# Scaled expert blocks scattered to the tokens' places by rows that carry their addresses, in a one-core fp32 attention and mixture-of-experts kernel

## The chip, the cores and the metric

The kernel runs on one core of a Trainium2 chip, as one launch. The metric is the device time in microseconds (us). A core has five engines that run side by side: TensorE (PE), VectorE (DVE), ScalarE (ACT), GpSimd (POOL) and SyncE (SP). They are ordered by semaphores alone. SP and ACT issue DMAs (rows named SPq and ACTq), and so does POOL, which also makes the indirect ones, whose row addresses come from a tile in SBUF.

## What is computed

Three residual layers on x of 16 x 64 tokens of width 512: cross attention to a context of 16 x 1601 rows, self attention with a low-rank correction, and a mixture of experts. The change is in the third:

```python
h = gelu(xf @ wg1 + bg1)                       # xf: the 1024 normalised tokens
probs = softmax((h @ wg2 + bg2)[:, :20])       # 20 experts
top_vals, top_idx = top_k(probs, 2)            # 2 experts for each token
gates = zeros((N, 20)).at[arange(N)[:, None], top_idx].set(top_vals)
def body(y, eb):
    We_e, be_e, g_e = eb
    return (y + g_e[:, None] * (xf @ We_e + be_e), None)
y, _ = scan(body, zeros, (We, be, gates.T))    # all in fp32
x = x + y
```

## The kernel before

All work of an engine is written out by hand in program order, with counted semaphores between the engines. Every fp32 product is made of three fp32r matmuls: an operand is split into a high part (an ACT copy) and a low part (a DVE subtraction, `rest` at L984 or `we_lo` at L1363), and `mm3` (L175 to L178) runs high-high, high-low and low-high.

**Cross attention** runs over the 16 batches in one pass (`cross`, 26.8 us a batch). SP loads the next batch's context into the single tile `craw` (L1650) as soon as DVE has read the former. Behind the context of batch 3, SP also clears two scratch tensors in HBM, `xg` and `yg` (4480 rows of 512 floats each): L1672 to L1677 write 20 pieces of 896 rows x 128 columns to `xg` and 12 pieces of 640 rows x 128 columns to the last rows of `yg`. The context of batch 4 stands behind them on SP's queue.

**Routing.** DVE picks two experts for each token, and its chain (L1384 to L1429) gives each of the 2 x 1024 (token, choice) pairs a slot: an expert n has the block of 128 slots n, and what does not fit goes to extra blocks, which 20 + `more` blocks hold in all (`more` is read from `ji`; in the profiled run there are 27 blocks). POOL then scatters the normalised token rows to their slots of `xg` by 16 indirect DMAs of 128 rows each (L1606), behind its low part of weight 2 (L1601).

**Expert blocks** (`block_of` on each engine). For block n, SP loads 128 token rows (`xi`, a ring of 6, L1754) and 1 MB of weights (`We`, a ring of 8 that runs ten blocks ahead, L1729 and L1732). PE transposes the rows of block n + 1 and then multiplies block n (12 matmuls of 512 columns). ACT does, in this order, the high part of the rows n + 1 (`xo`), the high part of the weights n + 2 (`we_hi`, 128 x 2048), the copy of the result n from PSUM to one of four buffers `yo` (in `xm` or `hT`), and issues its DMA to the block's 128 rows of `yg` (L963). DVE makes the two low parts; that of the weights, `we_lo`, reads two tiles of SBUF. POOL has nothing to do in this stage.

**The end.** All five engines meet at a barrier once the last stores have landed. POOL gathers each token's two result rows from `yg` by 16 indirect DMAs (L1624) into a ring `yga` of four tile pairs, DVE scales each by its gate and adds it to `x_sb` (L1478, L1481), and SP stores eight tiles of the result (L1795).

Of the kernel before, what the change touches and what calls it, by code (L numbers as in the profile page):

```python
# [17 lines left out]
def perceiver(nc, t, out):  # L18
# [5 lines left out]
    R, X, EARLY = 8, 6, 4  # L24
# [3 lines left out]
    with root:  # L28
# [3 lines left out]
        def sb(name, shape, dt=f32, es=root):  # L32
# [12 lines left out]
        acc = sb("acc", [128, NB, 8, 32])  # L45
        acct = acc[:, :, :, :].rearrange("p b t c -> p b (t c)")
        nm = sb("nm", [128, NB, 8])
        ls = sb("ls", [128, NB, 8])
# [73 lines left out]
        mf = sb("mf", [128, 8, 8])  # L122
# [12 lines left out]
        jc = sb("jc", [1, 15, E])  # L135
        jf = sb("jf", [1, 16])
        ji = sb("ji", [1, 16], i32)
        cs2 = sb("cs2", [128, 660])
        wr = sb("wr", [128, 6, 4, D])
        xi = sb("xi", [128, 6, D])  # L140
        xall = acc[:, :, :, :].rearrange("p b t c -> p (b t c)").rearrange("p (i n) -> p i n", i=8)
        p2 = [xall[:, 4:6, :].rearrange("p i n -> p (i n)").rearrange("p (t b k) -> p t b k", t=8, b=2), p2b[:, :, :, :]]
        bvr, g1raw = xall[:, 7, :], xall[:, 6, :].rearrange("p (k n) -> p k n", k=4)
        yo = [xm[:, 0, :], xm[:, 1, :], hT[:, 0:D], hT[:, D:T]]
        yga = wr[:, 0:2].rearrange("p r (a c) n -> p (r a) c n", c=2)
# [16 lines left out]
            v_gt p_gT v_gT p_be v_y d_sc a_we v_we a_wx v_wx p_xo a_xo v_xo p_y a_y v_out d_out  # L162
# [5 lines left out]
        d_ga = [sem(f"d_ga{i}") for i in range(4)]  # L168

        d_x, d_w = (S["d_x0"], S["d_x1"]), (S["d_w0"], S["d_w1"])  # L170
# [64 lines left out]
        def tensor(pe):  # L235
# [142 lines left out]
            pe.wait_ge(S["d_lora"], 16)  # L378
# [76 lines left out]
            weight_lora(0, 1, (d_raw[1], 16))  # L455
            pe.wait_ge(S["d_bro"], 16)
# [19 lines left out]
            weight_lora(1, 1, (d_raw[1], 32))  # L476
# [53 lines left out]
            def dense(what, i):  # L530
# [99 lines left out]
            pe.drain().then_inc(S["s_bar"], 1)  # L630
            pe.wait_ge(S["s_bar"], 2 * BARRIER)
# [18 lines left out]
        def bank_of(what, i):  # L650
            return bank[what, i]
# [26 lines left out]
        def scalar(act):  # L678
# [42 lines left out]
            def cross(seg):  # L721
                for n in range(16 * seg, 16 * seg + NB + 1):
# [46 lines left out]
            weight_hi(wh[0], raw[:, 0], (d_w[0], 16))  # L769
# [3 lines left out]
            weight_hi(wk, raw[:, 1], (d_w[1], 16))  # L773
            weight_hi(wv, raw[:, 0], (d_w[0], 32))
# [51 lines left out]
            def norm(n, i, dst):  # L826
                act.wait_ge(S["g_r"], n + 1)
                if n >= 12:
                    act.wait_ge(S["p_t2"], 14)
# [28 lines left out]
            act.wait_ge(d_raw[0], 32)  # L858
# [7 lines left out]
            act.wait_ge(d_raw[0], 48)  # L866
# [81 lines left out]
            def block_of(n):  # L948
# [27 lines left out]
            act.drain().then_inc(S["s_bar"], 1)  # L976
            act.wait_ge(S["s_bar"], 2 * BARRIER)


        def vector(dve):  # L980
# [22 lines left out]
            dve.wait_ge(S["d_m"], 32)  # L1003
# [52 lines left out]
            def make_cap(seg):  # L1056
                dve.wait_ge(S["d_cap"], 48 * (seg + 1))
# [831 lines left out]
```

## Time and profile before

| what | value |
|---|---|
| device time, median of 3 runs (lowest to highest) | 886.27 us (883.11 to 887.11) |
| device time of the profiled execution | 883.6 us |
| span of the profiled execution | 881.7 us |
| mean granted TensorE clock | 0.939 |
| PE, DVE, ACT, POOL busy | 764.9, 438.1, 386.8, 357.3 us |
| DMA traffic | 94.07 MB, mean 107 GB/s |

The span runs from the first to the last instruction of the profiled execution; 1.9 us of its device time lie outside. An engine's busy time is the sum over stages that are bound by different things, so a stage has to be looked at by itself. The stages: cross attention to about 522 us, self attention to about 702, routing and the scatter to about 751, expert blocks to about 850, the end to 881.7.

### The profile page before, as it was taken

How to read it: one execution, taken by the hardware profiler on the slowest of the kernel's cores; microseconds unless marked ns; L12 is line 12 of the kernel's file. 1: busy time of each engine (PE TensorE's matmuls, PEld its weight loads, DVE VectorE, ACT ScalarE, POOL GpSimd, SP SyncE). 2: the span in 40 equal slices, each digit the busy share in tenths (PEclk: the TensorE clock that was granted, in tenths of full speed). 3: DMA queues.
4: the chain of work that ended last, by engine and by line, in shares of the span. 5: the costliest groups of instructions: out<-in, count | busy, mean ns of one | idle time of the engine just before them, and what ended most of it. 6: DMA issues, size and time to landing. Idle time of an engine off the chain costs nothing.

```text
span 881.7 us, 16368 instructions
## 1 busy us (share of the span) xinstructions
PE 764.9 (87%) x6435; PEld 624.0 (71%) x6435; DVE 438.1 (50%) x907; ACT 386.8 (44%) x680; POOL 357.3 (41%) x367
## 2 busy tenths in 40 slices
PE   1999999889999999999999769799998537799950
PEld 0888888768888788887888557678887432687740
DVE  5724443444444444444444327434687363388844
ACT  1444552544444545445443414642344420488830
POOL 1228653754577545775455407300235127000025
PEclk9999999999999999999999989899999955799985
DMA  9201598221021110111100001101000474599837
GB/s 300 84 1 40 163 285 228 88 87 35 7 88 39 41 38 3 41 40 40 39 3 2 1 17 49 48 13 49 2 2 1 191 304 178 183 413 420 356 110 237
DMA packets 47862, 94.07 MB, mean 107 GB/s; under 512 B 3195, under 2 KB 29691, under 8 KB 43295
## 3 DMA queue, kind: packets, MB, share of 16 engines
q1 hardware_dynamic: 41326, 77.43, 25.1%
q0 software_dynamic: 2560, 8.39, 2.9%
q10 hardware_dynamic: 3888, 7.08, 2.1%
q8 instruction: 55, 0.90, 0.4%
q14 instruction: 33, 0.26, 0.1%
HBM read 66.41 MB, written 26.48 MB: 105 GB/s over the span
## 4 chain that ended last, share of the span: by engine, by line
PE 68%; ACT 7%; DVE 6%; SPq 5%; DMA 5%; issue 5%; POOL 3%; ACTq 1%; PEld 0%; POOLq 0%; DVEq 0%; PEldq 0%
PE bank L176 17%; PE bank L178 15%; PE bank L177 15%; PE bank L182 8%; SPq L1674 5%; PE bank L292 5%; PE bank L318 3%; ACT wh L680 3%; DMA xi<-scratch_xg 2%; PE bank L494 2%; POOL scratch_xg L1606 1%; ACT xu L680 1%; DMA wr<-scratch_yg,si 1%; POOL wr L1624 1%; PE bank L417 1%
## 5 line engine op out<-in xcount | busy, mean ns | idle before, releaser
L1532 POOL TENSOR_SCALAR pp<-pp,rl 128x416 f32<-128x416 f32 x128 | 190.4, 1501 | 174.2 <-DVE rl L1078 174.1
L1162 DVE CUSTOM_DVE_ANT_0 pp<-bank,cap 128x416 f32<-128x416 f32 x128 | 70.5, 589 | 106.2 <-PE bank L292 106.2
L754 ACT ACTIVATE pp<-pp,nm 128x416 f32<-128x416 f32 x128 | 81.2, 635 | 45.6 <-DVE nm L1162 45.3
L984 DVE TENSOR_TENSOR kk<-bank,kk 128x416 fp32r<-128x416 f32 x64 | 37.9, 592 | 124.8 <-ACT kk L680 124.8
L176 PE MATMUL bank<-chi,wk 128*128 128x416 f32 x256 | 95.5, 373 | 0.0
L177 PE MATMUL bank<-clo,wk 128*128 128x416 f32 x256 | 90.1, 352 | 0.0
L178 PE MATMUL bank<-chi,wk 128*128 128x416 f32 x256 | 90.1, 352 | 0.0
L176 PE MATMUL bank<-wv,chi 128*128 128x512 f32 x208 | 87.7, 422 | 0.0
L178 PE MATMUL bank<-wv,clo 128*128 128x512 f32 x208 | 82.2, 395 | 0.0
L177 PE MATMUL bank<-wv,chi 128*128 128x512 f32 x208 | 81.8, 393 | 0.0
L680 ACT ACTIVATE kk<-bank 128x416 fp32r<-128x416 f32 x64 | 33.1, 517 | 98.8 <-PE bank L178 98.8
L176 PE MATMUL bank<-wh,xu 128*128 128x512 f32 x152 | 63.7, 419 | 8.1 <-issue 4.7
L182 PE MATMUL bank<-cst,pp 128*128 128x128 f32 x512 | 68.5, 277 | 0.0
L182 PEld LDWEIGHTS bank<-cst,pp 128*128 128x128 f32 x512 | 57.8, 141 | 7.2 <-issue 3.3
L680 ACT ACTIVATE xu<-bank 128x512 fp32r<-128x512 f32 (+1 forms) x60 | 31.0, 541 | 72.1 <-PE bank L182 48.1
L177 PE MATMUL bank<-wh,xu 128*128 128x512 f32 x152 | 60.8, 400 | 0.0
L178 PE MATMUL bank<-wh,xu 128*128 128x512 f32 x152 | 60.7, 400 | 0.0
L1624 POOL DMA_INDIRECT wr<-scratch_yg,si x16 | 17.0, 1063 | 107.8 <-SPq L1791 103.3
L680 ACT ACTIVATE pt<-bank 128x512 f32<-128x512 f32 x64 | 38.0, 594 | 50.1 <-PE bank L182 50.1
L1132 DVE COPY pt<-bank 128x512 f32<-128x512 f32 x64 | 43.9, 686 | 22.6 <-PE bank L182 22.6
L176 PEld LDWEIGHTS bank<-wv,chi 128*128 128x128 f32 x208 | 39.4, 189 | 21.0 <-issue 14.4
L680 ACT ACTIVATE vv<-bank 128x512 f32<-128x512 f32 x52 | 31.0, 596 | 46.2 <-PE bank L178 46.2
(228 smaller groups left out, 1606.9 us busy)
## 6 DMA issues: line engine op xcount, KB each, us to landing
wr<-in_We SPq DMA_DIRECT2D x19, 1024.0 KB, 11.1
craw<-in_ctx SPq DMA_DIRECT2D x16, 832.0 KB, 4.4
scratch_xg<-zero SPq DMA_DIRECT2D x20, 448.0 KB, 6.3
raw<-in_We SPq DMA_DIRECT2D x8, 1024.0 KB, 11.3
xi<-scratch_xg SPq DMA_DIRECT2D x28, 256.0 KB, 10.1
scratch_yg<-zero SPq DMA_DIRECT2D x12, 320.0 KB, 5.2
scratch_yg<-xm ACTq DMA_DIRECT2D x14, 256.0 KB, 7.0
scratch_yg<-hT ACTq DMA_DIRECT2D x13, 256.0 KB, 6.6
```

Source lines behind the costliest of these rows:

```text
L176: pe.matmul(o, lhs[0], rhs[0], start=start, stop=False)
L177: pe.matmul(o, lhs[0], rhs[1], start=False, stop=False)
L178: return pe.matmul(o, lhs[1], rhs[0], start=False, stop=stop)
L182: last = pe.transpose(bank[0:n, k * 128:(k + 1) * 128], of(k), ident)
L292: last = pe.matmul(pb[3 + u][:, 0:CW], q[r, s, g, :], w[r, g, :], start=start, stop=stop)
L680: return act.activation(dst, src, ACT.Copy)
L754: act.activation(frame(p8), frame(p8), ACT.Exp, bias=bias, scale=-1.0, accum_out=total).then_inc(S["a_exp"], 1)
L984: return dve.tensor_tensor(dst, src, hi.bitcast(f32), ALU.subtract)
L1132: dve.tensor_copy(pt[:, p8 % 4, :, :].rearrange("p a c -> p (a c)"), pb[5][:, :]).then_inc(S["v_pt"], 1)
L1162: dve.tensor_tensor_reduce(out=frame(p8), in0=pb[3 + p8 % 2][:, 0:CW], in1=cap[:, :], scale=-1.0, scalar=nm[:, b, p8:p8 + 1] if seg else 3 ...
L1532: pool.tensor_scalar(frame(p8), frame(p8), rl[:, n % 2, p8:p8 + 1], None, ALU.mult).then_inc(S["g_pn"], 1)
L1674: sp.dma_start(t[name][first_ * 128:(first_ + n_) * 128, k * 128:(k + 1) * 128].rearrange("(a p) n -> p a n", p=128), zero[:, :].unsqueeze ...
```

## The change

- A row of `xg` and of the tile `xi` has 520 floats in place of 512. The eight more hold the token's two experts, its two gates, the two rows of the result at which its two products belong, and (for a slot that no token fills) a row of its own beyond the result's.
- `yg` goes; `ys` has 2048 rows for the 2 x 1024 products and 4480 behind them for the empty slots. The 12 clearing pieces for `yg` go. In their place one DMA from HBM to HBM writes the eight columns of 4480 rows of `xg` from a prepared array `empty`.
- For each block, POOL works out the gate and the row of each of its 128 tokens from the eight columns in five small instructions (`address`).
- ACT multiplies by the gate when it evicts the block from PSUM, and no longer stores. POOL stores, by an indirect DMA that scatters the 128 rows to `ys`.
- The barrier at the end goes, and so do the 16 gathers. SP waits for the last four scatters and then issues eight loads of 2 x 128 contiguous rows; DVE adds them without a factor.
- Several tiles of the self attention move within `acc`, because the eight token tiles there are now 520 wide, and some semaphores are shared. The instructions are otherwise the same.

```diff
-    R, X, EARLY = 8, 6, 4
+    R, X, EARLY, RW = 8, 6, 4, D + 8
...
-        yga = wr[:, 0:2].rearrange("p r (a c) n -> p (r a) c n", c=2)
+        yga = wr[:, 0:4].rearrange("p r (a c) n -> p (r a) c n", c=2)
...
# scalar, block_of(n)
-                copy(yo[n % 4], pb[3 + n % 2][:, :]).then_inc(S["a_y"], 1)
-                act.wait_ge(S["a_y"], n + 1)
-                act.dma_start(t["yg"][n * 128:(n + 1) * 128, :], yo[n % 4]).then_inc(d_yo[n % 4], 16)
+                act.wait_ge(S["g_ad"], n + 1)
+                act.activation(yo[n % 4], pb[3 + n % 2][:, :], ACT.Identity,
+                               scale=gd[:, n % 4, 0:1]).then_inc(S["a_y"], 1)
...
# vector, routing
-            chain(dve.tensor_copy(mf[:, :, :], mi[:, :, :]))
+            dve.wait_ge(S["d_gate"], 32)
+            dve.tensor_copy(xrow[:, :, D + 2:D + 4], mg[:, :, 0:2])
+            dve.tensor_copy(xrow[:, :, D + 4:D + 7], place_of)
+            chain(dve.tensor_copy(xrow[:, :, D:D + 2], mi[:, :, 0:2]))
...
# vector, the end
-                r = i % 4
-                dve.wait_ge(d_ga[r], 32 * (i // 4 + 1))
-                dve.scalar_tensor_tensor(out=x_sb[:, i, :], in0=yga[:, r, 0, :], scalar=mg[:, i, 0:1],
-                                         in1=x_sb[:, i, :], op0=ALU.mult, op1=ALU.add).then_inc(S["v_out"], 1)
...
+                dve.wait_ge(d_ga[i], 16)
+                for c in range(2):
+                    if c:
+                        dve.wait_ge(S["v_out"], 2 * i + 1)
+                    dve.tensor_tensor(x_sb[:, i, :], x_sb[:, i, :], yga[:, i, c, :], ALU.add).then_inc(S["v_out"], 1)
...
# gpsimd
+            def address(n):
...
+                r = n % X
+                pool.wait_ge(d_xi[r], 16 * (n // X + 1))
+                own.on(pool.tensor_scalar(eq[:, :], xi[:, r, D:D + 2], float(n) if n < E else jf[:, n - E:n - E + 1], None,
+                                          ALU.is_equal))
+                pool.wait_ge(own.sem, own.n)
+                own.on(pool.tensor_tensor(ad[:, :, :], xi[:, r, D + 2:D + 6].rearrange("p (a c) -> p a c", a=2),
+                                          eq[:, :].unsqueeze(1).to_broadcast([128, 2, 2]), ALU.mult))
+                pool.wait_ge(own.sem, own.n)
+                own.on(pool.tensor_tensor(gd[:, n % 4, :], ad[:, :, 0], ad[:, :, 1], ALU.add))
+                pool.wait_ge(own.sem, own.n)
+                own.on(pool.tensor_tensor(gd[:, n % 4, 1:2], gd[:, n % 4, 1:2], xi[:, r, D + 6:D + 7], ALU.add))
+                pool.wait_ge(own.sem, own.n)
+                if n >= 4:
+                    pool.wait_ge(d_yo[n % 4], 16 * (n // 4))
+                pool.tensor_copy(di[:, n % 4:n % 4 + 1], gd[:, n % 4, 1:2]).then_inc(S["g_ad"], 1)
+
+            def block_of(n):
+                address(n + 1)
+                pool.wait_ge(S["g_ad"], n + 1)
+                pool.wait_ge(S["a_y"], n + 1)
+                pool.indirect_dma_start(out=t["ys"][:, :],
+                                        out_offset=bass.IndirectOffsetOnAxis(ap=di[:, n % 4:n % 4 + 1], axis=0),
+                                        in_=yo[n % 4], in_offset=None).then_inc(d_yo[n % 4], 16)
...
# sync, cross attention
-        cleared = [("xg", 7 * j, 7) for j in range(5)] + [("yg", E + 5 * j, 5) for j in range(3)]
+        cleared = [(7 * j, 7) for j in range(5)]
...
+                        sp.dma_start(t["xg"][:, D:RW], t["empty"]).then_inc(S["d_z"], 16)
...
# sync, load_tokens(n) and the end
+                    sp.wait_ge(S["g_ad"], n - X + 1)
...
-            sp.drain().then_inc(S["s_bar"], 1)
-            sp.wait_ge(S["s_bar"], 2 * BARRIER)
+
+            for i in range(8):
+                sp.dma_start(yga[:, i], t["ys"][0:2 * T, :].rearrange("(c i p) n -> i p c n", c=2, i=8)[i]).then_inc(
+                    d_ga[i], 16)
```

On SP's queue in the cross attention, around the clearing, before:

```order
L1650 ISA
L1650 DMA craw<-in_ctx 128x1664
L1674 DMA scratch_xg<-zero 128x7x128 x20
L1674 DMA scratch_yg<-zero 128x5x128 x12
L1650 ISA
L1650 DMA craw<-in_ctx 128x1664
```

and in the changed kernel:

```order
L1677 ISA
L1677 DMA craw<-in_ctx 128x1664
L1701 DMA scratch_xg<-zero 128x7x128 x20
L1705 DMA scratch_xg<-in_empty 4480x8
L1677 ISA
L1677 DMA craw<-in_ctx 128x1664
```

Twelve pieces have left, one DMA of 4480 rows of 8 floats has come, and the context load of batch 4 follows it.

On POOL, from the scatter of the tokens on; the names in brackets are the semaphores that an instruction waits for (d_xi: the token rows have landed, g_ln: POOL's own last instruction, a_y: ACT's eviction, g_ad: `address`). Before:

```order
L1606 DMA scratch_xg<-acc,si 4480x512 x15
L1610 TENSOR_LOAD ji [waits v_ji]
L1610 ISA x2
L1612 COMPARE_AND_BRANCH x15
L1616 UNCONDITIONAL_BRANCH
L1624 DMA wr<-scratch_yg,si 128x512 [waits s_bar]
L1624 DMA wr<-scratch_yg,si 128x512 x7
```

and in the changed kernel, to the scatter of block 0:

```order
L1611 DMA scratch_xg<-acc,si 4480x520 x15
L1615 TENSOR_LOAD ji [waits v_ji]
L1615 ISA x2
L1623 TENSOR_SCALAR eq<-xi 128x2 [waits d_xi0]
L1626 TENSOR_TENSOR ad<-xi,eq 128x4 [waits g_ln]
L1629 TENSOR_TENSOR gd<-ad 128x2 [waits g_ln]
L1631 TENSOR_TENSOR gd<-gd,xi 128x1 [waits g_ln]
L1635 CAST di<-gd 128x1 [waits g_ln]
```

```order
L1623 TENSOR_SCALAR eq<-xi 128x2 [waits d_xi1]
L1626 TENSOR_TENSOR ad<-xi,eq 128x4 [waits g_ln]
L1629 TENSOR_TENSOR gd<-ad 128x2 [waits g_ln]
L1631 TENSOR_TENSOR gd<-gd,xi 128x1 [waits g_ln]
L1635 CAST di<-gd 128x1 [waits g_ln]
L1641 DMA scratch_ys<-xm,di 6528x512 [waits a_y,g_ad]
```

The first five of these instructions are `address(0)`, the next six are what every block then has: the address of block n + 1 and the scatter of block n.

On ACT, the first blocks (p_y: PE has finished the block, d_we: weights have landed), before:

```order
L680 ACTIVATE xm<-bank 128x512 [waits v_slot,p_y]
L963 DMA scratch_yg<-xm 128x512 [waits a_y]
L680 ACTIVATE xu<-bank 128x512 [waits p_y,p_xo]
L680 ACTIVATE wh<-wr 128x2048 [waits p_y,d_we3]
L680 ACTIVATE xm<-bank 128x512 [waits v_slot,p_y]
L963 DMA scratch_yg<-xm 128x512 [waits a_y]
```

and in the changed kernel:

```order
L969 ACTIVATE xm<-bank,gd 128x512 [waits g_ad,v_slot,p_y]
L683 ACTIVATE xu<-bank 128x512 [waits p_y,p_xo]
L683 ACTIVATE wh<-wr 128x2048 [waits p_y,d_we3]
L969 ACTIVATE xm<-bank,gd 128x512 [waits g_ad,v_slot,p_y]
L683 ACTIVATE xu<-bank 128x512 [waits p_y,p_xo]
```

The DMA has left ACT, and the eviction waits for POOL's `address` as well.

## Rows read from the trace of the kernel before

**Rows 1.** The page, part 4: the chain that ended last, share of the span by engine.

```profile
PE 68%; ACT 7%; DVE 6%; SPq 5%; DMA 5%; issue 5%; POOL 3%; ACTq 1%; PEld 0%; POOLq 0%; DVEq 0%; PEldq 0%
```

**Rows 2.** Timeline of SP's queue, 86 to 205 us: start, us, engine, line, operation, count.

```profile
98.31 30.70 SPq L1674 DMA_DIRECT2D scratch_xg<-zero  x20
129.06 15.11 SPq L1674 DMA_DIRECT2D scratch_yg<-zero  x12
```

**Rows 3.** Stage table: window, length, busy (count) PE, PEld, DVE, ACT, POOL, clock, DMA, GB/s.

```profile
109.60:136.40 26.80, 26.80 (x273) 22.45 (x269) 11.81 (x31) 13.08 (x28) 16.39 (x17) 1.00 1.04 287
136.40:167.70 31.30, 28.64 (x274) 23.98 (x269) 11.86 (x31) 12.60 (x28) 16.35 (x17) 0.95 0.60 184
```

**Rows 4.** Critical chain, 90 to 170 us: start, us, what; the context of batch 4.

```profile
144.35 7.33 DMA craw<-in_ctx
```

**Rows 5.** ACT's waits, 90 to 170 us: waiting, waited for, us in total, times, longest.

```profile
ACT chi L680 <- DMA craw<-in_ctx: 8.3, 1, 8.3
```

**Rows 6.** Timeline of ACT, from the first eviction of a block on.

```profile
760.94 0.60 ACT L680 ACTIVATE xm<-bank 128x512 f32<-128x512 f32 x1 [4.67 <-PE bank L178]
...
765.86 1.90 ACT L680 ACTIVATE wh<-wr 128x2048 fp32r<-128x2048 f32 x1
...
768.28 0.33 ACTq L963 DMA_DIRECT2D scratch_yg<-hT  x1
```

**Rows 7.** Critical chain, 700 to 882 us: DVE's cast, last scatter, last eviction, last addition.

```profile
717.13 3.47 DVE mf L1389
...
748.19 2.69 DMA scratch_xg<-acc,si
...
849.15 0.61 ACT hT L680
...
878.51 0.75 DVE x_sb L1481
```

**Rows 8.** Timeline of DVE, 782 to 800 us: the low parts of two weights.

```profile
784.52 2.29 DVE L1363 TENSOR_TENSOR wh<-raw,wh 128x2048 fp32r<-128x2048 f32 x1 [0.45 <-ACT wh L680]
...
787.87 2.29 DVE L1363 TENSOR_TENSOR wh<-wr,wh 128x2048 fp32r<-128x2048 f32 x1 [0.45 <-ACT wh L680]
```

**Rows 9.** Stage table of two stretches of the expert blocks.

```profile
782.00:815.00 33.00, 33.00 (x160) 26.26 (x159) 28.49 (x21) 28.80 (x30) 0.00 (x0) 1.00 1.03 418
833.00:850.00 17.00, 16.11 (x80) 12.88 (x78) 11.43 (x9) 11.17 (x13) 0.00 (x0) 1.00 0.28 104
```

**Rows 10.** Timeline of PE, 815 to 834 us: the token transposes and their waits.

```profile
825.16 0.66 PE L182 MATMUL bank<-cst,xi 128*128 128x128 f32 x4 [0.34 <-DMA xi<-scratch_xg]
...
828.93 0.66 PE L182 MATMUL bank<-cst,xi 128*128 128x128 f32 x4 [0.36 <-DMA xi<-scratch_xg]
```

**Rows 11.** Line 1568, a POOL operation: ns min/median/max, first and last start.

```profile
L1568 POOL TENSOR_TENSOR nbias<-nbias,rstd x16: 189/189/603, 534.6 to 701.2; 128x1 f32<-128x1 f32 x16
```

**Rows 12.** Timeline of DVE and POOL, 640 to 646 us, around the longest of those.

```profile
643.97 0.55 POOL L1567 TENSOR_TENSOR rstd<-rstd,cst 128x1 f32<-128x1 f32 x1 [1.16 <-DVE nbias L1238]
644.47 0.68 DVE L984 TENSOR_TENSOR g<-acc,g 128x512 fp32r<-128x512 f32 x1
644.60 0.60 POOL L1568 TENSOR_TENSOR nbias<-nbias,rstd 128x1 f32<-128x1 f32 x1
```

**Rows 13.** Timeline of POOL and DVE, 846 to 882 us: two of the 16 gathers.

```profile
857.28 0.75 DVE L1478 SCALAR_TENSOR_TENSOR x_sb<-wr,mg,x_sb 128x512 f32<-128x512 f32 x1 [9.11 <-DMA wr<-scratch_yg,si]
857.47 1.38 POOL L1624 DMA_INDIRECT wr<-scratch_yg,si  x1 [0.30 <-issue]
...
864.43 0.94 POOL L1624 DMA_INDIRECT wr<-scratch_yg,si  x1 [0.30 <-issue]
864.78 0.75 DVE L1478 SCALAR_TENSOR_TENSOR x_sb<-wr,mg,x_sb 128x512 f32<-128x512 f32 x1 [3.17 <-DMA wr<-scratch_yg,si]
```

**Rows 14.** DMA issues of the span: form, count, KB each, median us to landing.

```profile
craw<-in_ctx SPq DMA_DIRECT2D x16, 832.0 KB, 4.4
```

More of the change, by code:

```diff
@@ L44, in perceiver @@
         iota20 = cst[:, 160:180]
[L45 to L48, printed above, removed]
+        acc = sb("acc", [128, NB * 256 + 2 * NB * 8])
+        acct = acc[:, 0:NB * 256].rearrange("p (b n) -> p b n", b=NB)
+        nm, ls = [acc[:, NB * 256 + j * 128:NB * 256 + (j + 1) * 128].rearrange("p (b h) -> p b h", b=NB)
+                  for j in range(2)]
         raw = sb("raw", [128, 2, 4, D])
@@ L167, in perceiver @@
         d_yo = [sem(f"d_yo{i}") for i in range(4)]
-        d_ga = [sem(f"d_ga{i}") for i in range(4)]
-        d_x, d_w = (S["d_x0"], S["d_x1"]), (S["d_w0"], S["d_w1"])
+        d_ga = [sem(f"d_ga{i}") for i in range(8)]
+        d_x = (S["d_x0"], S["d_x1"])
         d_raw = (S["d_raw0"], S["d_raw1"])
@@ L827, in norm @@
                 act.wait_ge(S["g_r"], n + 1)
-                if n >= 12:
+                if n == 11:
+                    act.wait_ge(S["v_v2"], 8)
+                elif n == 12:
+                    act.wait_ge(S["v_g1"], 1)
+                elif n >= 13:
                     act.wait_ge(S["p_t2"], 14)
@@ L1418, in vector @@
                                             op1=ALU.add))
-            chain(dve.tensor_tensor(jc[:, :, :], ob[0:1, 20:40].unsqueeze(1).to_broadcast([1, 15, E]),
+            chain(dve.tensor_tensor(jc[:, :, :], ob[:, 20:40].unsqueeze(1).to_broadcast([128, 15, E]),
                                     jg.rearrange("p (j e) -> p j e", e=E), ALU.is_le))
@@ L1429, in vector @@
             dve.tensor_copy(si[:, :, :], sf[:, :, :]).then_inc(S["v_slot"], 1)
-            own.on(dve.tensor_scalar(ji[:, 0:15], jf[:, 0:15], float(E - 1), None, ALU.min))
+            chain(dve.tensor_scalar(jf[:, 0:15], jf[:, 0:15], float(E - 1), None, ALU.min))
+            own.on(dve.tensor_copy(ji[:, 0:15], jf[0:1, 0:15]))
             dve.wait_ge(own.sem, own.n)
@@ L1607, in gpsimd @@
                                             out_offset=bass.IndirectOffsetOnAxis(ap=si[:, c, i:i + 1], axis=0),
-                                            in_=xall[:, i, :], in_offset=None).then_inc(S["d_sc"], 16)
+                                            in_=xrow[:, i, :], in_offset=None).then_inc(S["d_sc"], 16)
             pool.wait_ge(S["v_ji"], 1)
             more = pool.value_load(ji[0:1, 15:16], min_val=0, max_val=X8)
+            def address(n):
+                if n >= LAST:
+                    return
+                r = n % X
[20 more added lines that the diff above has]
+                                        in_=yo[n % 4], in_offset=None).then_inc(d_yo[n % 4], 16)
+            address(0)
+            for n in range(E):
+                block_of(n)
             for j in range(X8):
@@ L1613, in gpsimd @@
                 guards[-1].__enter__()
[L1614 removed]
+                block_of(E + j)
             while guards:
                 guards.pop().__exit__(None, None, None)
[L1617 to L1629 removed]
+        cleared = [(7 * j, 7) for j in range(5)]
+        Z_ALL = 16 * (4 * len(cleared) + 1)
         def sync(sp):
@@ L1841 @@
     cs2[:, 360:660] = _np.repeat(_np.arange(15), 20)
+    place = cs2[:, 660:684].reshape(128, 8, 3)
+    for c in range(2):
+        place[:, :, c] = _np.arange(128)[:, None] + 128 * _np.arange(8) + 1024 * c
+    empty = _np.zeros((35 * 128, 8), _np.float32)
+    empty[:, 6] = 2048 + _np.arange(35 * 128)
     wqkv, bqkv = v["L0_attn_w_qkv"], v["L0_attn_b_qkv"]
```

103 lines of the change are left out of this document (44 added, 59 removed).

## The prediction

> **What bounds the kernel now.** I read the chain that ended last first, then the stages it passes. TensorE holds 68% of it [rows 1], but the change leaves TensorE's work as it is, so I look for the places where the chain leaves PE. There are three: 5% of the span on SP's queue, the expert blocks, and the end.
>
> *The clearing.* SP issues 20 pieces to xg in 30.7 us and 12 to yg in 15.1 us [rows 2], and the DMA engines are full meanwhile (share 1.04 at 287 GB/s [rows 3]). The context of batch 4 is issued behind them at 144.35 and lands 7.33 us later, at 151.7 [rows 4]; ACT waits 8.3 us for it [rows 5]. PE loses less: that batch takes 31.3 us against 26.8 for its neighbour [rows 3], that is 4.5. So 8.3 - 4.5 = 3.8 us of such a delay cost PE nothing.
>
> *The expert blocks.* The first eviction starts at 760.94 [rows 6], the last at 849.15 [rows 7]: 26 intervals in 88.2 us, 3.39 each. Two limits lie on top of each other. ACT and DVE set a pace of 3.35 (the two weight operations of rows 8 start that far apart). And a block moves 1.05 MB of weights, 0.26 of tokens and 0.26 of results, 1.57 MB; at the 418 GB/s of full DMA engines [rows 9] that is 3.76 us, the pace at which PE's transposes wait for tokens late in the stage (825.16 to 828.93 [rows 10]). Weights loaded ahead hide that limit for two thirds of the blocks. PE alone could do 3.22: 80 matmuls, five blocks, in 16.11 us [rows 9].
>
> *The end* takes 881.7 - 849.15 - 0.6 = 32.0 us from the last eviction's end.
>
> **Part 1, the clearing.** The 20 xg pieces have 20 x 896 = 17,920 rows of 512 bytes, 1.71 ns each at 30.7 us. The new DMA adds 4480 rows of 32 bytes. The trace has no such transfer. Lower bound: by its bytes nothing; nearest row: the same 1.71 ns a row, 7.7 us; upper bound: twice that, 15.4, because it both reads and writes HBM. The xg rows are now 2080 bytes apart, which may slow their 512-byte pieces, by nothing to a quarter (estimate). With the nearest row, SP is through at 98.3 + 30.7 + 7.7 = 136.7, and the context lands, 7.3 us later as before [rows 4], at 144.0. It would cost PE nothing up to 151.7 - 4.5 = 147.2. Gain 4.5, and no more is to be had there. Upper end: 98.3 + 38.4 + 15.4 = 152.1, 7.8 later than before, all of it paid: 7.8 lost. I take -4.5, since 3.2 us of reserve are left. The Trainium skill, DMA: Bandwidth & Descriptors, Specifications, speaks against this: below 512 bytes the DMA engine does a read-modify-write. It gives no price for one, and no row here shows it; the sum by it would be that of the upper end.
>
> **Part 2, routing.** DVE's cast took 3.47 us [rows 7] because POOL's subtraction for weight 2 was under way; the two new small copies stand in front of it and partly vanish in that wait. Bounds 0 to 0.5; I take +0.4, two small DVE operations. The extra waits of moved tiles are for events that lie steps back: nothing.
>
> **Part 3, the expert blocks.** ACT loses a DMA issue of 0.33 us [rows 6] and its wait, so its pace drops from 3.35 to about 2.95, below PE's 3.22. That gives at most what DMA leaves, for the last weights still arrive at DMA's pace: 0 to -1. What comes is POOL's work. A small operation takes 0.19 [rows 11], and the next that depends on it starts 0.08 after its end (643.97 + 0.55 = 644.52 to 644.60 [rows 12]); I take 0.25 for each of the five, so `address` takes 1.25. A scatter takes 0.30 + 0.96 = 1.26 like the gathers [rows 13]. Sum 2.5, under 3.22: were POOL alone, it would hide. It isn't. In rows 12 a POOL operation begun while DVE works on two SBUF tiles ends at 645.20, just after DVE (645.15), in 0.60 instead of 0.19. In rows 13 an indirect DMA begun under such a DVE operation (to 858.03) ends 0.82 later, while one that has begun 0.35 us before DVE is not disturbed. So each of POOL's six starts needs a moment in which DVE isn't in a two-tile operation; `we_lo` is one, and lasts 2.29 per block [rows 8].
>
> Bounds for the pace. Best phase: only the scatter's 0.82 lies under `we_lo`; 2.29 + 1.25 + 0.15 = 3.7. Worst: nothing does; 2.5 + 2.3 = 4.8. What does the program do? Say POOL finishes an `address` at 0 and ACT has waited for it. ACT evicts (0.5), copies rows (0.5) and the weights (1.9, all three by rows 6, the small ones overlapping by 0.1): `we_lo` runs from 3.0 to 5.3. POOL scatters to 1.3 and makes the next address by 2.55 (a short block: ACT takes it up at 3.0). The next scatter starts at 2.85, before DVE, and is done at 3.8. Then the address after next: its first operation is held to 5.3, the others follow, but the next `we_lo` is due at 6.0, when three or four are done, and holds the rest to 8.3; the address is ready at about 8.6. Two blocks take 8.6, 4.3 each. From there it repeats. The first three intervals have little of this: 3 x 3.2 + 23 x 4.3 = 108.5 against 88.2: **+20.3**. Ends: 3.7 gives 94.7 (+6.5), 4.8 gives 120 (+32). DMA isn't the limit at 4.3 (1.57 MB in 4.3 us is 366 GB/s). Queued behind POOL's wait is only POOL; those who wait for it are ACT's eviction, then PE's third block after, through the two result banks.
>
> **Part 4, the end.** After the last eviction POOL may still have to scatter the block before, make an address and scatter the last: 1.3 to 3.8, I take 3.2. Landing 0.3 + 2.7, from the scatter to xg [rows 7]. Eight loads: 512 KB land first after about 3.6 (832 KB take 4.4 [rows 14]); all 4.2 MB need 10.0 at 418 GB/s, so DVE's 16 additions at 0.72 (0.68 [rows 12] and a wait), 11.5, end last. The last store takes 881.7 - 879.26 = 2.4 [rows 7]. Sum 3.2 + 3.0 + 0.3 + 3.6 + 11.5 + 2.4 = 24.0: **-8.0**, range -5 to -10. Hidden: the barrier, and the loads behind the additions.
>
> **Sum**: -4.5 + 0.4 + 20.3 - 8.0 = +8.2. The profiled 883.6 (1.9 outside its span) becomes 891.8. The median of the runs is 2.7 above that execution, so 886.3 + 8.2 = 894.5.
>
> **Rivals.**
> *POOL hides.* If the small operations slip between DVE's, POOL's 2.5 stays under 3.22 and DMA sets the end of the stage: -0.5 there, and the last scatter starts at once, -9.9 at the end. Sum -14.5: 871.8. For it: the sum of 2.5, and an idle DVE for 1 us a block. Against: rows 12 and 13. It decides for the gain from a POOL chain of about 0.7 us on, where I have 1.25.
> *Best phase.* The pace settles at 3.7: +6.5. Sum -5.6: 880.7.
> *No overlap at all.* Pace 4.8, +32, sum +20: 906. The Trainium skill, SBUF — State Buffer, section "SBUF: two separate sides", says that GpSimd cannot write descriptors while DVE holds the shared port in a two-port mode. Were it so for `we_lo` too, the 0.82 could not lie under it and this rival would hold; the undisturbed issue of rows 13 says otherwise.
> *The clearing runs late.* The upper end of part 1, on top of the forecast: +7.8 in place of -4.5, 906.8. It decides from an SP queue that is through later than 139.9.
>
> **Chances.** Forecast (pace 4.0 to 4.6, 887 to 902) 0.50; POOL hides 0.20; best phase 0.12; no overlap 0.08; late clearing 0.10. A measurement can tell about 0.5%, 4.4 us. Faster: the 0.20 and most of the 0.12, 0.31. The same: some 0.14 of the forecast's lower edge and the rest, 0.15. Slower: 0.54. The range leaves out about 0.15 and takes in the hidden POOL's edge and both late ends: 870 to 908. The likeliest case's own is 887 to 902.
>
> **What the new profile should show.** SP through with the clearing near 137 and no wait of ACT for the context. In the expert blocks POOL near full, its small operations in two kinds (0.19, and up to 2.3 when held), evictions alternating between about 3 and 5.7 us, ACT waiting for POOL, DMA share under 1. The end 24 us long, with DVE adding without gaps. An even pace near 3.4 with no ACT wait for POOL would prove part 3 wrong; a context that lands after 147 proves part 1 wrong.

## The result, and the profile after

The changed kernel takes 907.8 us (median of four runs, 904.7 to 911.4), the kernel before 886.7 beside it: a ratio of 1.025, with a 95% interval of 1.019 to 1.031. Two of the four runs lie near 905 and two near 911; nothing here shows what separates them, and the profile is of the fastest. The profiled execution took 904.7 us with a span of 902.9, against 883.6 and 881.7. The prediction was 894.5: the right side, but a growth of 8.2 us where 21 were measured, at the upper edge of the range. The two spans differ by 21.2 us. To find where, I cut both at the first and the last eviction of an expert block:

| stretch of the span, us | before | after | difference | forecast |
|---|---|---|---|---|
| up to the first eviction | 760.94 | 757.66 | -3.3 | -4.1 |
| first to last eviction, 26 intervals | 88.2 | 119.5 | +31.3 | +20.3 |
| start of the last eviction to the end | 32.6 | 25.7 | -6.8 | -8.0 |

**The chain.** The page of after, part 4. GpSimd (POOL) stood at 3% of it before [rows 1]:

```profile
PE 71%; POOL 13%; issue 6%; DVE 5%; DMA 2%; ACT 2%; PEld 0%; POOLq 0%; SPq 0%; DVEq 0%; PEldq 0%; ACTq 0%
```

**The clearing.** Timeline of SP's queue in after (start, us, engine, line, operation, count), and the stage of the batch behind it (window, length, busy and count of PE, PEld, DVE, ACT, POOL, then PE's granted clock, DMA share and GB/s):

```profile
98.14 34.05 SPq L1701 DMA_DIRECT2D scratch_xg<-zero  x20
132.24 1.65 SPq L1705 DMA_DIRECT2D scratch_xg<-in_empty  x1
134.08 4.61 SPq L1677 DMA_DIRECT2D craw<-in_ctx  x1
```

```profile
135.70:162.20 26.50, 26.50 (x264) 22.19 (x255) 11.83 (x30) 12.79 (x29) 16.09 (x16) 1.00 0.43 114
```

SP is through at 133.9. ACT's wait of 8.3 us for the context [rows 5] is gone, and the batch takes 26.5 us where it took 31.3 [rows 3].

**The expert blocks.** Timeline of DVE, ACT and POOL in after, two blocks from one free scatter to the next. L1641 is the scatter, L1623 to L1635 the five address steps, L1368 the low part of a weight (`we_lo`), L969 the eviction:

```profile
837.87 1.08 POOL L1641 DMA_INDIRECT scratch_ys<-xm,di  x1 [0.52 <-POOL di L1635]
838.53 1.91 ACT L683 ACTIVATE xu<-wr 128x2048 fp32r<-128x2048 f32 x1
...
839.03 0.21 POOL L1623 TENSOR_SCALAR eq<-xi 128x2 f32<-128x2 f32 x1
...
840.13 0.18 POOL L1635 CAST di<-gd 128x1 uint32<-128x1 f32 x1
...
840.43 0.69 ACT L969 ACTIVATE hT<-bank,gd 128x512 f32<-128x512 f32 x1
840.47 2.29 DVE L1368 TENSOR_TENSOR xu<-wr,xu 128x2048 fp32r<-128x2048 f32 x1 [1.11 <-ACT xu L683]
840.83 2.89 POOL L1641 DMA_INDIRECT scratch_ys<-xm,di  x1 [0.52 <-POOL di L1635]
...
843.44 2.29 DVE L1368 TENSOR_TENSOR wh<-wr,wh 128x2048 fp32r<-128x2048 f32 x1
843.79 2.01 POOL L1623 TENSOR_SCALAR eq<-xi 128x2 f32<-128x2 f32 x1
...
846.70 0.18 POOL L1635 CAST di<-gd 128x1 uint32<-128x1 f32 x1
847.00 0.69 ACT L969 ACTIVATE hT<-bank,gd 128x512 f32<-128x512 f32 x1 [3.59 <-POOL di L1635]
847.40 1.08 POOL L1641 DMA_INDIRECT scratch_ys<-hT,di  x1 [0.52 <-POOL di L1635]
```

A scatter that starts before `we_lo` takes 1.08 us. The one at 840.83 starts 0.36 us after `we_lo` began, and takes 2.89: it ends 0.96 us after DVE does. The compare at 843.79 starts 0.35 us after the next `we_lo`, and takes 2.01 instead of 0.21. Undisturbed, POOL gets from one scatter to the next in 2.96 us (837.87 to 840.83), and disturbed in 6.57. The pair is 9.53, or 4.77 a block; with two easy intervals at the start and a cheaper pair at the end the mean is 4.60. ACT waits for POOL's address meanwhile, in 11 long waits of together 39.6 us (waiting, waited for: us in total, times, longest):

```profile
ACT hT L969 <- POOL di L1635: 21.6, 6, 3.7
ACT xm L969 <- POOL di L1635: 18.0, 5, 3.7
```

The stage table of a longer stretch, with PE's clock at 0.95, shows that no other resource is full: POOL is busy for 52.8 of 65 us, and the rest are the gaps within its own cycle (0.52 before the scatter and five of about 0.08, 0.90 in each of 13.6 cycles). PE has 50.7, and DMA is at 0.88 where it was 1.03 [rows 9].

```profile
782.00:847.00 65.00, 50.71 (x224) 39.69 (x224) 40.48 (x28) 39.74 (x41) 52.84 (x82) 0.95 0.88 307
```

**The end**, timelines of ACT, POOL, SP's queue and DVE in after:

```profile
877.18 0.69 ACT L969 ACTIVATE hT<-bank,gd 128x512 f32<-128x512 f32 x1 [1.86 <-POOL di L1635]
...
880.60 1.08 POOL L1641 DMA_INDIRECT scratch_ys<-hT,di  x1 [0.52 <-POOL di L1635]
...
887.52 10.81 DVE L1487 TENSOR_TENSOR x_sb<-x_sb,wr 128x512 f32<-128x512 f32 x16 [11.49 <-DMA wr<-scratch_ys]
```

```profile
883.63 4.01 SPq L1822 DMA_DIRECT2D wr<-scratch_ys  x8
```

The 16 additions run without gaps, as forecast, and end at 898.3; 4.6 us pass from there to the end of the span, when the last store has landed.

### The profile page after: what moved, and what is told of

Read it like the earlier page. It is cut to its first block, busy times and chain, and to the rows that moved or that the text cites. A ratio compares the mean times of both kernels' runs of the same rounds, so it can differ in the third digit from the quotient of the medians.

```text
span 902.9 us, 16536 instructions
## 1 busy us (share of the span) xinstructions
PE 770.3 (85%) x6435; PEld 627.9 (70%) x6435; DVE 437.9 (49%) x910; ACT 389.1 (43%) x680; POOL 442.0 (49%) x518
## 3 DMA queue, kind: packets, MB, share of 16 engines
q1 hardware_dynamic: 40126, 77.97, 26.7%
## 4 chain that ended last, share of the span: by engine, by line
PE 71%; POOL 13%; issue 6%; DVE 5%; DMA 2%; ACT 2%; PEld 0%; POOLq 0%; SPq 0%; DVEq 0%; PEldq 0%; ACTq 0%
PE bank L181 18%; PE bank L183 16%; PE bank L182 16%; PE bank L187 8%; POOL scratch_ys L1641 5%; PE bank L297 5%; PE bank L323 3%; POOL eq L1623 3%; PE bank L499 2%; POOL scratch_xg L1611 2%; DVE x_sb L1487 1%; PE bank L422 1%; POOL gd L1629 1%; PE bank L511 1%; PE bank L529 1%
## 5 line engine op out<-in xcount | busy, mean ns | idle before, releaser
L757 ACT ACTIVATE pp<-pp,acc 128x416 f32<-128x416 f32 x128 | 81.3, 636 | 47.7 <-DVE acc L1167 47.5
L181 PE MATMUL bank<-wh,xu 128*128 128x512 f32 x152 | 64.5, 424 | 22.3 <-DVE xu L989 12.5
L989 DVE TENSOR_TENSOR xu<-bank,xu 128x512 fp32r<-128x512 f32 (+1 forms) x60 | 35.7, 613 | 54.2 <-ACT xu L683 54.1
L1137 DVE COPY pt<-bank 128x512 f32<-128x512 f32 x64 | 43.9, 686 | 25.7 <-PE bank L187 25.7
```

Source lines behind the costliest of these rows:

```text
L181: pe.matmul(o, lhs[0], rhs[0], start=start, stop=False)
L757: act.activation(frame(p8), frame(p8), ACT.Exp, bias=bias, scale=-1.0, accum_out=total).then_inc(S["a_exp"], 1)
L989: return dve.tensor_tensor(dst, src, hi.bitcast(f32), ALU.subtract)
L1137: dve.tensor_copy(pt[:, p8 % 4, :, :].rearrange("p a c -> p (a c)"), pb[5][:, :]).then_inc(S["v_pt"], 1)
```

## The experiments

Two theories stood after the traces. **T**: POOL's own cycle is the pace of the expert blocks, 2.96 us by itself and some 1.8 more for each `we_lo` that it runs into. **Rivals**: the length of POOL's chain without any hold, the landing of scatters and weights, or the hand-over between POOL and ACT. All spans are cut as above. Each ratio is to runs of the kernel before that were made beside that kernel; their medians are 886.7 for after, 884.3 for e1 to e4, 886.4 for e5 to e7 and 884.1 for e8 to e10. The changed kernel was not run again beside the experiments, so differences from it carry some 2 to 3 us of doubt.

| kernel | median us | ratio to before (95%) | 26 intervals | mean | last eviction to end |
|---|---|---|---|---|---|
| before | 886.7 | | 88.2 | 3.39 | 32.6 |
| after | 907.8 | 1.025 (1.019 to 1.031) | 119.5 | 4.60 | 25.7 |
| e1, low part from PSUM | 872.6 | 0.986 (0.983 to 0.989) | 88.3 | 3.40 | 24.3 |
| e2, low part in four | 876.2 | 0.990 (0.987 to 0.993) | 89.6 | 3.44 | 25.7 |
| e3, clearing part alone | 881.5 | 0.997 (0.995 to 0.999) | 88.2 | 3.39 | 34.3 |
| e4, addresses worked out once | 871.8 | 0.985 (0.983 to 0.988) | 87.5 | 3.37 | 23.7 |
| e5, address two ahead | 904.9 | 1.023 (1.020 to 1.025) | 116.4 | 4.48 | 28.3 |
| e6, e1 with four more steps | 892.0 | 1.009 (1.005 to 1.012) | 104.0 | 4.00 | 26.8 |
| e7, e1 for even blocks alone | 883.4 | 0.998 (0.995 to 1.000) | 96.5 | 3.71 | 26.7 |
| e8, e4 again | 871.3 | 0.985 (0.983 to 0.988) | 87.3 | 3.36 | 24.2 |
| e9, e4 with the low part in four | 870.9 | 0.985 (0.983 to 0.987) | 87.1 | 3.35 | 24.1 |
| e10, e4 with stores by ACT | 873.4 | 0.987 (0.984 to 0.989) | 87.3 | 3.36 | 25.6 |

### e1: the hold taken away, the work kept

```diff
+                if n < 3:
...
+                    return
-                dve.tensor_tensor(wsplit[n % 3][1], wraws[n % R], wsplit[n % 3][0].bitcast(f32),
+                dve.tensor_tensor(wsplit[n % 3][1], wraws[n % R],
+                                  pb[7][:, :].unsqueeze(1).to_broadcast([128, 4, D]),
                                   ALU.subtract).then_inc(S["v_we"] if n < E else S["v_wx"], 1)
```

> The changed kernel, with one operand of VectorE's low-part instruction moved out of SBUF: from the fourth weight on it reads a PSUM bank where it read the high part in SBUF (so the low parts are wrong numbers; size and count of the work are as before). In the changed kernel a GpSimd instruction that touches SBUF while that 2.29 us instruction runs takes 2.0 to 2.9 us instead of 0.2 to 1.1. Theory (the two engines hold each other up at SBUF, and the scatter starts 0.36 us after the low part begins instead of before it): no GpSimd row of the expert blocks above 1.3 us, blocks at 3.2 to 3.6 us each instead of 4.60, the 26 intervals shorter by 26 to 36 us, total 870 to 880. Rival A (the length of GpSimd's own chain of seven dependent steps, 3.5 us when nothing holds it, plus the hand-overs, sets the pace): 4.3 to 4.6, total 898 to 906. Rival B (scatter landings or the weight loads set it): no change, 903 to 911.

Blocks take 3.40 us in the mean, as before, and the total is 35 us below the changed kernel's. One address and its scatter in e1, and the `we_lo` (now L1372) that runs meanwhile, timeline of POOL and DVE:

```profile
802.26 0.21 POOL L1628 TENSOR_SCALAR eq<-xi 128x2 f32<-128x2 f32 x1
...
802.67 2.29 DVE L1372 TENSOR_TENSOR wh<-raw,bank 128x2048 fp32r<-128x2048 f32 x1 [0.32 <-ACT wh L683]
...
803.35 0.18 POOL L1640 CAST di<-gd 128x1 uint32<-128x1 f32 x1
804.32 1.08 POOL L1646 DMA_INDIRECT scratch_ys<-hT,di  x1 [0.78 <-ACT hT L969]
```

`we_lo` is as long as before, 2.29 us, and only one of its inputs has changed its place. No POOL row is long, neither the cast nor the scatter that start under it, and the scatter now waits for ACT, not the other way round. POOL's 28 chains are all still there, so their length alone isn't the cause; nor are the landings. Rivals A and B fall. The mean of 3.40 is made of blocks of 3.2 and, late in the stage, seven of 3.7 to 4.4, where before had 3.34 and then up to 3.77.

### e2: the same work in shorter instructions

```diff
+                for k in range(4):
+                    ins = dve.tensor_tensor(wsplit[n % 3][1][:, k, :], wraws[n % R][:, k, :],
+                                            wsplit[n % 3][0][:, k, :].bitcast(f32), ALU.subtract)
+                ins.then_inc(S["v_we"] if n < E else S["v_wx"], 1)
```

> The changed kernel, with the low part (2.29 us for 128x4x512) issued as four instructions of 128x512, about 0.6 us each; nothing else. Theory (GpSimd is held until the running VectorE instruction ends): it then waits at most 0.6 us at a time, a scatter takes at most 1.7 us and the compare at most 0.9, pace 3.5 to 4.0, total 876 to 892. If VectorE keeps the port across instructions that stand back to back, the holds stay at 1.8 us and nothing changes: 903 to 911. Rival (GpSimd's chain or the landings): 903 to 911 too, but with short rows.

One held scatter and one held step of e2:

```profile
800.44 1.34 POOL L1643 DMA_INDIRECT scratch_ys<-hT,di  x1 [0.52 <-POOL di L1637]
...
802.19 0.51 POOL L1628 TENSOR_TENSOR ad<-xi,eq 128x4 f32<-128x4 f32 x1
```

The holds shrink from 1.8 us to mostly 0.3 or 0.4 (0.7 at most), the blocks to 3.44, just under the range expected: between two DVE instructions that stand back to back POOL gets its turn. Four pieces take 2.50 us where one took 2.29. This version does all the work, and it is 1.0% faster than the kernel before (876.2 against 884.3).

### e3: the clearing part alone

```diff
                     if seg == 0 and b == 2:
-                        for name, first_, n_ in cleared:
+                        for name, first_, n_ in cleared[0:5]:
...
+                    if seg == 0 and b == 12:
+                        for name, first_, n_ in cleared[5:8]:
```

> The kernel before, with the twelve zero pieces of the result scratch issued after the fourteenth context load instead of in one row with the other twenty after the fourth. They are as many, and the rest is the kernel before. The changed kernel is without them, and its first 757 us came out 3.28 us shorter than before (6.24 us at 442 us, of which about 3 were lost again at the end of cross attention, where TensorE's granted clock dipped). Theory (they stand before the fifth context load on SyncE's queue and nothing else notices them): 4 to 6.5 us shorter at 442 us, total 880 to 884. Rival (the gain needs the pieces gone, because their transfer takes the same room wherever it stands): within 1 us of the kernel before, 883 to 888.

Moved, the twelve pieces cost nothing where they now are (timeline of SP's queue in e3):

```profile
377.34 13.68 SPq L1681 DMA_DIRECT2D scratch_yg<-zero  x12
```

Two rows of PE, the first product of the output projection, of before and of e3, show what it gives:

```profile
498.74 0.50 PE L176 MATMUL bank<-wh,oh 128*128 128x512 f32 x1 [2.80 <-DVE oh L984]
```

```profile
495.06 0.50 PE L176 MATMUL bank<-wh,oh 128*128 128x512 f32 x1 [2.79 <-DVE oh L984]
```

It is 3.7 us, a little less than the 4 expected, and 4.5 if one allows for e3's context load, which SP issued 0.8 us later than before's (98.75 against 97.93). The profiled execution keeps little of it: its first eviction is 1.5 us earlier than before's, since 2.1 are lost in front of the row scatters (see the last section), and 1.7 more are lost at the end (34.3 against 32.6), in code that is the same. It is the slowest of ten runs. The median falls by 2.8, and the interval of the ratio (0.995 to 0.999) leaves out 1: the rival falls, by a small margin.

### e4: the whole chain taken off GpSimd

```diff
+            act.wait_ge(S["d_sc"], 256)
+            act.dma_start(ex[:, :, :], t["xg"][:, D:RW].rearrange("(n p) c -> p n c", p=128)).then_inc(S["d_ex"], 16)
...
+            chain(dve.tensor_tensor(eq[:, :, :], ex[:, :, 0:2], bid[:, :].unsqueeze(2).to_broadcast([128, NBK, 2]),
+                                    ALU.is_equal))
...
             def block_of(n):
-                address(n + 1)
-                pool.wait_ge(S["g_ad"], n + 1)
                 pool.wait_ge(S["a_y"], n + 1)
                 pool.indirect_dma_start(out=t["ys"][:, :],
```

The multiplication, the two additions and the cast follow in the same manner, each once for all 35 blocks. The loads of the token rows leave out the eight columns and no longer wait for POOL, so e4 changes more than one thing at once; the single cause rests on e1 and e5 to e7.

> The changed kernel with gates and places worked out once: one load brings the eight extra columns of all 35 blocks after the row scatters, VectorE computes all gates and places in five small instructions, and GpSimd only scatters. The block loads leave the extra columns out. Theory (GpSimd's chain under the hold sets the pace): 35 fewer chains of 1.0 to 3 us; a scatter may still be held behind a low part (2.9 us), but nothing stands behind it any more, so blocks at 3.2 to 3.5 us, first eviction later by 1 to 3 us (the extra load of about 2 us and some 1.5 us on VectorE), total 870 to 880. Rival A (the scatter's hold itself sets the pace): 4.0 or more, total above 888. Rival B (landings): 4.6, 903 to 911.

Timelines of DVE and of POOL in e4:

```profile
757.46 0.31 DVE L1483 TENSOR_TENSOR jc<-hT,sl 128x140 f32<-128x140 f32 x1
757.80 0.23 DVE L1485 TENSOR_TENSOR gd<-jc 128x70 f32<-128x70 f32 x1
```

```profile
781.53 1.99 POOL L1639 DMA_INDIRECT scratch_ys<-hT,di  x1 [1.20 <-ACT hT L973]
784.71 1.99 POOL L1639 DMA_INDIRECT scratch_ys<-xm,di  x1 [1.20 <-ACT xm L973]
787.90 1.99 POOL L1639 DMA_INDIRECT scratch_ys<-xm,di  x1 [1.20 <-ACT xm L973]
```

The five instructions take 1.2 us for all blocks together, behind a wait of 2.1 us for their load. The scatter is still held, to 1.8 or 2.0, in nearly every block, and yet the blocks come every 3.19 us here, since POOL has 1.2 us to spare behind it. Rival A falls. At 871.8 us this is 36 us below the changed kernel and 12.5 below the kernel before beside it.

### e5: the same steps, one block earlier

```diff
-                if n >= 4:
-                    pool.wait_ge(d_yo[n % 4], 16 * (n // 4))
+                if n >= 8:
+                    pool.wait_ge(d_yo[n % 4], 16 * (n // 4 - 1))
...
-                address(n + 1)
+                address(n + 2)
```

> The changed kernel with the address steps two blocks ahead of their scatter instead of one (rings of eight for gates and places, one more token load at the end); the same instructions. Two theories agree so far. Theory T (throughput): GpSimd's own cycle is the pace. Without holds one cycle is 2.93 us (scatter 1.08, five small steps with their gaps 1.35, 0.5 from the last step to the next scatter), and each cycle or so meets one low part and loses up to 1.8: twice 2.93 and two holds of 1.8 are 9.5 us a pair, and 9.54 was measured. Then working further ahead changes little: 4.3 to 4.8 a block, total 896 to 911. Theory L (hand-over): ScalarE's wait for the address of the next block (39.6 us in 11 waits) closes a loop, and working two ahead opens it: 3.3 to 3.7 a block, total 871 to 882.

T's side: 904.9 us, 4.48 a block. Timeline of POOL in e5:

```profile
803.75 2.89 POOL L1641 DMA_INDIRECT scratch_ys<-xm,di  x1 [0.52 <-POOL di L1635]
...
807.29 2.19 POOL L1629 TENSOR_TENSOR gd<-ad 128x2 f32<-128x2 f32 x1
```

Another step is hit, but for as long, and the mean falls by 0.12 only. POOL isn't late by its place in a loop: its cycle and the holds fill the time.

### e6: the cycle made longer without a hold

```diff
+                for _ in range(2):
+                    own.on(pool.tensor_scalar(eq[:, :], xi[:, r, D:D + 2], float(n) if n < E else jf[:, n - E:n - E + 1], None,
+                                              ALU.is_equal))
+                    pool.wait_ge(own.sem, own.n)
...
```

> The kernel of the first experiment (low part from PSUM, so no holds; its low parts are wrong numbers), with the first four of the five address steps done twice. That adds four times 0.27 us, 1.1 us a block, to GpSimd and no hold. Theory T: GpSimd's cycle is 2.93 + 1.1 = 4.0, above the 3.4 of the rest, so 4.0 to 4.2 a block and a total of 888 to 895, against 872.6 of the first experiment. If only being held matters and length doesn't (the rest has room): 3.4 and 871 to 875.

Measured 892.0 and 4.00 us a block. Two scatters of e6 stand 4.07 apart:

```profile
799.83 1.08 POOL L1647 DMA_INDIRECT scratch_ys<-hT,di  x1 [0.53 <-POOL di L1641]
...
803.90 1.08 POOL L1647 DMA_INDIRECT scratch_ys<-hT,di  x1 [0.52 <-POOL di L1641]
```

So length counts as a hold does, once the sum exceeds what the rest needs (3.2 to 3.8 in e1).

### e7: the hold in every second block

```diff
-                if n < 3:
+                if n < 3 or n % 2:
```

> The kernel of the first experiment with the PSUM operand for even blocks alone; the odd ones read the SBUF high part again (low parts of the even ones are wrong numbers). Theory T: a pair costs twice 2.93 and one hold of 1.8 at most, 7.7 us, so 3.6 to 3.9 a block where it starved before and a total of 877 to 886. If the first hold of a pair is what sets off the second (phase), taking one away takes both: 3.4 and 871 to 876.

Measured 883.4 and 3.71 a block. Timeline of POOL in e7, one cycle free (2.95) and one held (4.77), 7.72 the pair, as expected:

```profile
802.60 1.08 POOL L1646 DMA_INDIRECT scratch_ys<-hT,di  x1 [0.52 <-POOL di L1640]
...
805.55 2.90 POOL L1646 DMA_INDIRECT scratch_ys<-xm,di  x1 [0.52 <-POOL di L1640]
...
810.32 1.07 POOL L1646 DMA_INDIRECT scratch_ys<-xm,di  x1 [0.52 <-POOL di L1640]
```

With e1, e6, e7 and the changed kernel the price adds up: 2.96 + 0 stays hidden, 2.96 + 1.1 gives 4.00, half a hold 3.71, a hold in each cycle 4.60 (means of 26; in the steady part 4.07, 3.86 and 4.77).

### e8 to e10: what is left in the batched kernel

> The batched kernel of the fourth experiment once more, on the chip and beside the two that follow, to compare them with. 871.8 us was measured; 869 to 874 again.

871.3 us; it repeats.

e9 has the edit of e2 on top of e4.

> The batched kernel with the low part in four instructions of 128x512. In the batched kernel a scatter is still held by 0.9 us in every block (about 1.9 to 2.0 against 0.96 us), but GpSimd has 1.2 to 1.9 us to spare behind it. Theory T (a hold costs something only where GpSimd's cycle is the longest): scatters of 1.2 us or less, and the total unchanged within 1.5 us, or up to 2 us longer, since the four pieces take 2.50 us where one took 2.29. If the hold itself still costs in the batched kernel: 2 to 6 us shorter.

870.9 us, the same. The scatters are short, 1.00 for most and up to 1.47 for the others, somewhat above the 1.2 expected:

```profile
793.63 1.00 POOL L1641 DMA_INDIRECT scratch_ys<-hT,di  x1 [2.19 <-ACT hT L973]
```

That a hold off the path costs nothing is thus shown twice, in e4 and here.

```diff
-            for i in range(8):
-                sp.wait_ge(S["v_out"], 2 * i + 2)
-                sp.dma_start(out.rearrange("(i b) q d -> i (b q) d", b=2)[i], x_sb[:, i, :]).then_inc(S["d_out"], 16)
...
+            for i in range(8):
+                act.wait_ge(S["v_out"], 2 * i + 2)
+                act.dma_start(out.rearrange("(i b) q d -> i (b q) d", b=2)[i], x_sb[:, i, :]).then_inc(S["d_out"], 16)
```

> The batched kernel with the eight stores of the output issued on ScalarE's queue, which is idle there, instead of SyncE's, which has issued the eight loads just before. In the changed kernel the last store landed about 4.6 us after the last add, where the prediction had counted 2.4. If they queue behind the loads on the same queue, this takes 1 to 2.5 us off the end; if the time is the stores' own way, nothing (within 0.5 us).

e10 moves the stores to the end of ACT's program. 873.4 us: not the gain of 1 to 2.5 us that was expected, and by its ratio hardly distinguishable from e8. The trace shows two effects against each other. The last rows of DVE in e10:

```profile
866.27 1.42 DVE L1508 TENSOR_TENSOR x_sb<-x_sb,wr 128x512 f32<-128x512 f32 x2 [1.08 <-DMA wr<-scratch_ys]
868.61 1.42 DVE L1508 TENSOR_TENSOR x_sb<-x_sb,wr 128x512 f32<-128x512 f32 x2 [0.93 <-DMA wr<-scratch_ys]
```

The last store lands 2.5 us after the last addition (872.5 - 870.0) where e8 needs 4.1 (869.7 - 865.6). But the additions now wait for most of the loads, about 1 us each towards the end, and stretch from 11.7 us to 14.8. So 1.6 us are gained and 3.1 lost. My reading, which no run isolates: on one queue the stores go behind the loads and let them through, on two queues they take bandwidth from them.

## Why the prediction was wrong

**Part 1, the clearing: right, with two sizes off.** The 32-byte rows cost 1.65 us of SP's queue, not 7.7, and not the 15.4 of the upper bound: 4480 rows at 0.37 ns, about a fifth of the 1.71 that I took from the nearest row. So the price of a row does not carry over from the zero pieces, which take 1.5 to 1.7 us each with 896 rows; what sets it was not tried. The zero pieces at the new distance cost 34.05 instead of 30.70, within the nothing to a quarter that I allowed. SP was through at 133.9 (136.7 forecast), the late rival (139.9 on) is out, and the batch gained 4.8 (4.5 forecast); e3 isolates 3.7 to 4.5. The other terms of the first stretch are in the last section.

**Part 2, routing: right.** From DVE's first instruction on the experts' scores to the first scatter of token rows it is 16.30 us, against 16.27 before (709.34 to 725.64, and 712.63 to 728.90): nothing, at the lower bound of 0 to 0.5. The long wait has moved from the cast to one of the new copies (3.32 us). That scatter starts 3.26 us earlier than before and the first eviction 3.28, so nothing is lost between them either.

**Part 3, the expert blocks: the mechanism right, POOL's own time too small, and with it the step on its phase wrong.** The step reads: "The next scatter starts at 2.85, before DVE". Counted from the end of the address before, as there, the trace has the scatter at 3.48 and `we_lo` at 3.12 (840.83 and 840.47, less 837.35). DVE was forecast well (3.0). POOL was 0.63 late: 0.52 instead of 0.30 us pass between the cast and the indirect DMA that reads its result, twice (0.44); the scatter takes 1.08, not 0.96 (0.12); the five steps with their gaps take 1.36, not 1.25 (0.11, less 0.04 that the forecast had rounded up). So it starts behind `we_lo`, not 0.15 ahead of it, and is held for 1.8 us in place of not at all. A pair costs 9.53 instead of 8.6.

The holds as such are not what is missing: the forecast's pair has twice 2.51 of POOL's own time (0.30 + 0.96 + 1.25) and 3.6 of holds, all of them on address steps; the trace's has twice 2.96 and 3.61 of holds (1.81 on a scatter, 1.80 on a compare). The term that was mis-sized is POOL's own cycle, 2.51 for 2.96. That is 0.9 a pair, and over the twelve pairs of the stage about the 11 us by which the blocks missed (119.5 against 108.5).

What I had treated as a question of phase is, by e5 to e7, better said as a sum: POOL's cycle of 2.96 and one hold for each `we_lo`. The bound "no overlap" (4.8, 906 us) was built on such a sum, and it is the case that came: 4.77 in the steady pairs. That the number fits so well is luck: its 2.5 and 2.3 stand for 2.96 and 1.8. I had given it 0.08 because the forecast's walk beat DVE by 0.15 us; a margin smaller than the error of its terms should not have carried half the chance.

**The port.** The Trainium skill, SBUF — State Buffer, section "SBUF: two separate sides", says that a VectorE operation with two SBUF inputs holds the shared port pair for its whole length against GpSimd operations that read SBUF. The rows of after agree (2.01 and 2.89 us for 0.21 and 1.08), and e1, where one input comes from PSUM, has none of it. The Trainium skill, SBUF — State Buffer, section "Who interferes with whom", infers that writing descriptors isn't hit by such an operation; here the indirect DMA is held when it starts after `we_lo` has begun, and not when it starts before. In the held ones 0.96 us remain after DVE's end, out of 1.08, which fits a wait at the start, though no run separates the parts of the instruction. The undisturbed issue of rows 13, with which I had argued against "no overlap", had begun ahead of DVE's operation, and so said nothing of one that begins behind it.

**Part 4, the end: right, by terms that erred both ways.** From the last eviction's end to the end of the last scatter 3.8 us (3.2 forecast); to the issue of the loads 1.95 (3.3); first load 3.9 (3.6); additions 10.8 (11.5); last store 4.6 (2.4). Sum 25.0 against 24.0. e10 says where the store's missing 2.2 went, as far as it can be said: with the stores on a queue of their own it takes 2.5, and the additions pay for it.

**The rivals.** "POOL hides" has now been seen, as e1: 872.6 us, where it was priced at 871.8, though against the kernel before beside it that is -11.7 and not -14.5. Its condition, a chain of about 0.7 us, was not tried. e1 keeps the chain of 1.3 us and has no hold, and its cycle of 2.96 is under the 3.2 of the rest; e4 has no chain and a hold of some 1 us in nearly each block, and hides that. "Best phase", an even pace of 3.7, did not come: the intervals are 2.96 and 6.57.

## What to carry to other kernels

Work given to GpSimd beside VectorE operations with two SBUF inputs should be budgeted as its own cycle plus up to one hold per such operation, and compared with the pace of the rest; here, whether it stayed hidden was a matter of that sum, and working one block further ahead (e5) gave back 0.12 us of 1.2 a block. Small per-block steps that need data known beforehand are better done once for all blocks (1.2 us on VectorE in e4 against 28 chains of 1.3 us on GpSimd and their holds), and where GpSimd must stay busy, cutting the long VectorE instruction in four (e2) gave nearly all of the loss back. Of the parts of this change, the end (-7 to -9 us in after, e1, e4, e8 and e9) and the clearing (-3 to -5) were worth having all along; only the address steps on GpSimd in every block spoiled them.

## What the runs showed that I had not expected

**A loss of TensorE's clock that moves.** The profiles of after, e8, e9 and e10 have a granted clock of 1.00 from 162 to 195 us and reach the output projection at 492.1 to 492.9; then the clock is 0.79 from 490 to 506. Those of e1 and e4 to e7 have 0.90 in the first stretch, reach it at 495.2 to 495.9, and have 1.00 in the second. Here is the second stretch in after, and in before the stretch with the same work:

```profile
487.90:505.50 17.60, 12.87 (x112) 9.77 (x111) 4.65 (x11) 4.07 (x9) 6.26 (x5) 0.81 0.00 1
```

```profile
494.20:508.60 14.40, 9.67 (x111) 7.51 (x111) 4.64 (x11) 4.07 (x9) 6.18 (x5) 1.00 0.00 1
```

PE's busy time grows by 3.2 us, and so does the stretch: it worked for a while at the lower of its two levels, 1.2 instead of 2.4 GHz, after an idle time of 2.8 us that before has as well, though before keeps its full clock there. So the six microseconds that after is ahead at 492.5 are three by the first scatter. Either loss came to about 3 us, and none of these profiles had neither; what decides which was not tried. e2 and e3 had part of both (0.95 and 0.89), and start the row scatters at 727.7 and 727.4 us, 1.2 us or more later than after, e1 and e4 to e9 (725.2 to 726.2). e10 starts them at 727.2, though it had the one loss alone; why is open. A gain read off in front of such a stretch is therefore not yet a gain in the end.

**A held GpSimd instruction shows only in its own length.** No row names VectorE as what it waited for; the profile counts the hold as busy time. In after POOL is "busy" for 52.8 of 65 us, and some 25 of these are holds (65 / 4.77 = 13.6 cycles with 1.8 each). A median length beside the maximum, or the shortest row of the same form, is what gives it away.
